# Routed experts in a transformer chain: items of one expert with both choices, against items of one choice at two experts

## The chip, the cores and the metric

The kernel runs on 1 core of a Trainium2 chip. TensorE (PE in the profile) does matrix products, VectorE (DVE), ScalarE (ACT) and GpSimd (POOL) do the rest, and SyncE (SP) and POOL issue the DMAs. The metric is device time in microseconds; the kernel before takes 2097.72 us, the median of three runs.

## The reference, cut to what matters

Four entries of 512 tokens with 128 features pass through a chain of attention and feed-forward blocks. The block that is changed is the second feed-forward, a mixture of eight experts with two choices per token and a capacity of 320 tokens for each choice at each expert:

```python
T = B * S                                      # 2048 tokens
probs = softmax(xf @ gate_w.T)
top_p, top_i = top_k(probs, 2)
w = top_p / (sum(top_p) + 1e-9)
capacity = int(1.25 * T / 8)                   # 320
oh = one_hot(top_i, 8)
my_rank = sum((cumsum(oh, axis=0) - 1) * oh, -1)   # rank within the choice
keep = my_rank < capacity
comb = einsum('tk,tke->te', w * keep, oh)
for e in range(8):
    y = silu(xf @ gate_proj_w[e].T) * (xf @ up_proj_w[e].T) @ down_proj_w[e].T
    out = out + comb[:, e:e + 1] * y
x = x + out
```

Behind it comes cross attention ("unit 3" in the kernel), which begins with a layer norm of x, entry by entry.

## The kernel before, in words

The whole chain is one program. `program_order` writes the order of all steps by hand as nested lists, and `interleaved` weaves neighbouring items into one flat list. Every engine walks the same list and does its own part of each step, so a step's place in the list sets its place on each engine. Buffers are rings (`T.slot`, `T.freed`); the ring `prob` has six buffers, `wide` (PSUM) three, `ys` three.

Tokens are routed through DRAM. After the gate of an entry, POOL scatters its normed tokens (`scatter`, L2181) to rows of `slots_in`, where expert e owns `ES` = 640 rows, 320 for first and 320 for second choices; tokens over capacity go to spare rows. When all four entries are scattered, the experts run as eight items, one expert each: SP loads the 640 rows (`slots_in`, L783), PE turns them (`f1_turn`), PE multiplies with the gate and up weights in four tiles of 320 columns (`f1_hidden`), ACT applies silu (L2016), DVE multiplies (L1671), PE projects down (`f1_down`, five blocks of 128 rows, two matmuls each), DVE copies the result to SBUF (L1678) and SP stores it to `slots_out` (L789). When all eight are stored, POOL gathers for entry 0, tile by tile, the rows of first and second choice (`gather`, L2201), and DVE adds them, scaled by their share, to x (`f1_add`, L1692), two adds per tile. Entries 1 to 3 follow inside the items of unit 3 (`prepare` in `cross_steps`), eight gathers and eight adds each. For entry 0, PE waits for the last gather before it runs some matmuls on an identity (`stay_awake`) and then turns the normed tokens. In front of the experts, the order has the keys and values of unit 3 for all entries (`kv_project`, DVE L1408 to L1439).

## Time and profile before

| | |
|---|---|
| times of three runs | 2097.72, 2096.28, 2105.15 us |
| median | 2097.72 us |
| the profiled execution: span of its instructions | 2100.9 us |
| PE busy | 1827.5 us, 87% |
| DVE busy | 1415.5 us, 67% |
| ACT busy | 1067.7 us, 51% |
| POOL busy | 784.6 us, 37% |

The profile comes from one more execution, for which the span from first to last instruction is listed and no other time. Busy time is summed over the whole program; the routed experts and what follows them lie between about 415 and 570 us. A matmul of 32-bit numbers shows as two records with a weight load (PEld) each. In the order of time, a row gives the start, the duration, the engine and line, what is written from what, the count, and in brackets how long the engine had been idle and what ended the idling.

### The profile page before, as it was taken

Reading aid. Unit: us, or ns where it says so; the run is one execution under the profiler, and the core shown is the slowest. Engines: PE = TensorE matmul, PEld = TensorE weight load, DVE = VectorE, ACT = ScalarE, POOL = GpSimd, SP = SyncE. Lnnn points to the kernel's source line nnn. Section 1 sums busy time; section 2 is a strip of 40 time slices with the busy share of each in tenths; the row PEclk is TensorE's granted clock in tenths of the full one; section 3 lists DMA queues with packets and bytes.
Section 4 is the critical chain, followed back from the end, with each engine's and each line's share of the span. In section 5 each row is a group of like instructions: output and inputs, shape, how many; then the busy total and the mean of one; then the engine's idle time right before and its main releaser. Section 6 shows DMA issues by size and latency. Waiting matters only on the chain. (4 is left out here: it accounts for less than half of the span.)

```text
span 2100.9 us, 34690 instructions
## 1 busy us (share of the span) xinstructions
PE 1827.5 (87%) x13011; PEld 1120.1 (53%) x13011; DVE 1415.5 (67%) x3427; ACT 1067.7 (51%) x1523; POOL 784.6 (37%) x1131
## 2 busy tenths in 40 slices
PE   5978998594777898899999999999999989989978
PEld 4557664373544444564544565644555554456557
DVE  8667776543676877864577885567786467787475
ACT  2655655131453566564466566366656446656510
POOL 4423324403624453431455342245443155443130
PEclk9999999597787898998999999999999999999989
DMA  7443333121000000141000033000014000003200
GB/s 227 111 137 101 109 104 97 63 69 39 21 1 13 1 1 13 37 110 43 16 1 1 1 93 84 28 1 1 1 44 120 14 16 2 1 26 99 52 1 21
DMA packets 69995, 100.91 MB, mean 48 GB/s; under 512 B 17126, under 2 KB 35438, under 8 KB 69188
## 3 DMA queue, kind: packets, MB, share of 16 engines
q1 hardware_dynamic: 60612, 90.01, 14.9%
q0 software_dynamic: 9216, 8.69, 1.6%
q8 instruction: 104, 1.70, 0.3%
q14 instruction: 63, 0.52, 0.1%
HBM read 52.43 MB, written 12.38 MB: 31 GB/s over the span
## 5 line engine op out<-in xcount | busy, mean ns | idle before, releaser
L1806 DVE TENSOR_REDUCE maxima<-wide 128x2 f32<-128x512 f32 (+3 forms) x512 | 406.1, 819 | 134.2 <-PE wide L836 130.7
L2042 ACT ACTIVATE prob<-wide 128x768 f32<-128x768 f32 (+1 forms) x384 | 332.2, 881 | 149.7 <-PE wide L836 149.4
L1965 ACT ACTIVATE prob<-wide 77x1024 f32<-77x1024 f32 x256 | 257.8, 1017 | 89.8 <-PE wide L836 86.5
L836 PE MATMUL wide<-q_g 32*128 32x256 f32 (+3 forms) x2048 | 268.5, 394 | 37.5 <-ACT prob L2042 18.1
L2284 POOL TENSOR_SCALAR_AFFINE_SELECT prob<-prob 128x256 f32<-128x256 f32 (+1 forms) x384 | 184.9, 487 | 296.4 <-ACT prob L2042 294.6
L1482 DVE TENSOR_REDUCE maxima<-wide 128x8 f32<-128x616 f32 x256 | 202.9, 795 | 110.7 <-PE wide L836 106.7
L836 PEld LDWEIGHTS wide<-q_g 32*128 32x128 f32 x2048 | 140.0, 188 | 205.6 <-issue 100.1
L2106 POOL TENSOR_TENSOR rstd<-moments,cst 128x4 f32<-128x4 f32 x88 | 90.4, 1027 | 360.7 <-DVE moments L1370 173.8
L1886 ACT ACTIVATE q_g<-wide 128x1024 fp32r<-128x1024 f32 x128 | 131.1, 1024 | 179.3 <-PE wide L836 177.4
L1886 ACT ACTIVATE q_g<-acc 128x512 fp32r<-128x512 f32 x192 | 114.5, 596 | 144.0 <-PE acc L836 139.0
L2191 POOL DMA_DIRECT2D masked_k<-kx x224 | 121.2, 546 | 177.4 <-PE wide L836 176.3
L836 PE MATMUL wide<-kx,q_g 128*128 128x312 f32 x512 | 178.0, 413 | 9.7 <-DVE maxima L1482 7.1
L836 PE MATMUL wide<-masked_q,masked_k 109*77 109x512 f32 x448 | 154.1, 429 | 11.9 <-DMA masked_q<-q_g 5.6
L836 PE MATMUL wide<-bias_q,ident_b 128*128 128x312 bf16 x448 | 134.8, 308 | 21.5 <-DVE maxima L1482 17.5
L836 PE MATMUL wide<-cst,hid 128*128 128x128 f32 x768 | 117.3, 293 | 30.6 <-DVE maxima L1482 9.8
L836 PE MATMUL acc<-prob,vx 77*32 77x512 f32 x1024 | 139.2, 616 | 0.7 <-ACT prob L1965 0.6
L836 PE MATMUL acc<-prob,A 128*32 128x512 f32 (+3 forms) x1408 | 136.1, 461 | 0.0
L836 PE MATMUL acc<-cst,hid 128*128 128x128 f32 x768 | 120.7, 281 | 13.8 <-DVE hid L1473 13.8
L836 PE MATMUL wide<-causal_b,ident_b 128*128 128x128 bf16 (+1 forms) x768 | 126.6, 248 | 0.0
L836 PE MATMUL wide<-hT,ffn_w 128*128 128x512 f32 x256 | 120.9, 597 | 3.9 <-DVE hid L1816 3.9
L836 PEld LDWEIGHTS wide<-cst,hid 128*128 128x128 f32 x768 | 91.5, 149 | 55.0 <-issue 21.1
L836 PEld LDWEIGHTS wide<-kx,q_g 128*128 128x128 f32 x512 | 101.4, 203 | 17.8 <-DVE maxima L1482 9.1
(253 smaller groups left out, 3096.1 us busy)
## 6 DMA issues: line engine op xcount, KB each, us to landing
masked_q<-q_g SPq DMA_DIRECT2D x448, 64.0 KB
masked_q<-mask_l SPq DMA_DIRECT2D x84, 308.0 KB
masked_k<-kx POOLq DMA_DIRECT2D x224, 19.5 KB, 1.9
A<-in_w SPq DMA_DIRECT2D x2, 2048.0 KB, 12.2
unit_w<-in_unit_w SPq DMA_DIRECT2D x8, 448.0 KB, 3.9
ffn_w<-in_ffn_w SPq DMA_DIRECT2D x4, 768.0 KB, 4.7
slots_in<-v_third SPq DMA_DIRECT2D x1, 2560.0 KB, 12.6
prob<-slots_in SPq DMA_DIRECT2D x8, 320.0 KB, 3.1
```

The costliest lines, as they stand in the source:

```text
L836: return e.matmul(out, lhsT, rhs, start=start, stop=stop, is_transpose=turn)
L1482: e.tensor_reduce(maxima[g % 2][:, 2 * half:2 * half + 2, :], v, AX.X, ALU.max, negate=True).then_inc(*made("max", ("free", tile)))
L1806: e.tensor_reduce(top[:, t, h], v[:, :, at0:at0 + P * t + P], AX.X, ALU.max, negate=True).then_inc(*made("max", *([("free", tile)] if t == ...
L1886: return e.activation(out, src, ACT.Copy, bias=0.0, scale=1.0)
L1965: e.activation(p[0:SC, :], s[0:SC, :], ACT.Exp, bias=0.0, scale=1.0).then_inc(*made("exp", pb, ("free", tile)))
L2042: e.activation(pv, sv, ACT.Exp, bias=0.0, scale=8 ** -0.5).then_inc(*made("exp", pb, ("free", tile)))
L2106: e.tensor_tensor(rstd[T.slot("rstd", held)][:, :], mo[:, 8 * NI:9 * NI], const("minus_half"), ALU.pow).then_inc(*made("rstd", held))
L2191: e.dma_start(masked_k[at][0:HR, :, i, :].bitcast(F32), kx[HR * i:HR * i + HR, i, 2 * half:2 * half + 2, SK * b:SK * b + SK].bitcast(F32)) ...
L2284: e.affine_select(out=v, in_=v, compare_op=ALU.is_ge, fill=0.0, base=0, pattern=[[0, many], [1, P]], channel_multiplier=-1).then_inc(*made ...
```

## The change: what it does

Items are grouped by choice. Items 0 to 3 hold first choices, items 4 to 7 second choices, and each holds two experts (`pair_of`), 320 rows of one expert on partitions 0 to 63 and 320 of the other on 64 to 127. `slots_in` and `slots_out` become two DRAM tensors each, one per choice. The scatters of an entry do the four first choices and then the four second ones. The first-choice rows of all entries are gathered behind the stores of items 0 to 3 and added to x in the order of the steps behind item 5 and later; the second choices follow where both were before. The sizes of loads, stores and matmuls change as the diff shows.

```diff
-SLOTS = E8 * ES
-SPARE = 2 * B * S
+HALF = P // 2
+SLOTS = E8 * CAP
+SPARE = B * S
...
-    every += [[[[("slots_in", x)]], [[("f1_turn", x)]], [[("f1_hidden", x, c, h)] for c in range(2) for h in range(2)],
+    sparse = [[[[("slots_in", x)]], [[("f1_turn", x)]], [[("f1_hidden", x, c, e)] for c in range(2) for e in range(2)],
                [[], [("f1_down", x)], [("f1_out", x)]]] for x in range(E8)]
-    every += [[[]]] * 3
-    every += [[[[("gather", 0, i)] for i in range(NI)]]]
+    sparse += [[[[]]] for _ in range(4)]
+
+    for b in range(B):
+        first_choice = sparse[E8 // 2 + 3 + b]
+        first_choice[0] = beside(first_choice[0], [[("gather", b, 0, i)] for i in range(NI)])
+        sparse[E8 // 2 + 4 + b][0] = beside(sparse[E8 // 2 + 4 + b][0], [[], [], [], [("f1_add", b, 0, 0)]])
+    sparse[-1][0] = beside([[("gather", 0, 1, i)] for i in range(NI)], sparse[-1][0])
+    every += sparse
...
+        def pair_of(x8, e):
+            return 2 * (x8 % (E8 // 2)) + e
...
+                    for k in range(2):
+                        e.dma_start(slots_in[k][0:SLOTS, :].rearrange("(p c) d -> p c d", p=P),
+                                    blank.unsqueeze(1).broadcast_to([P, SLOTS // P, D])).then_inc(*landed("clear_slots"))
...
+                for w in need(*[("scattered", b, x8 // (E8 // 2)) for b in range(B)], T.freed("prob", ("xs", x8))):
+                    e.wait_ge(*w)
+                e.dma_start(to[0:HALF, 0:ES], slots_of(x8, 0, slots_in)).then_inc(*landed(f"load_slots{x8}"))
+                e.dma_start(to[HALF:P, 0:ES], slots_of(x8, 1, slots_in)).then_inc(*landed(f"load_slots{x8}", ("xs", x8)))
...
+                of = ys[T.slot("ys", ("ys", x8))]
+                e.dma_start(slots_of(x8, 0, slots_out), of[0:HALF, :]).then_inc(*landed(f"store_slots{x8}"))
+                e.dma_start(slots_of(x8, 1, slots_out), of[HALF:P, :]).then_inc(
                     *landed(f"store_slots{x8}", ("stored_slots", x8), ("free", ("ys", x8))))
...
-                s, v = wide[T.slot("wide", tile)], xT[T.slot("xT", held)][:, EH * h:EH * h + EH]
+                s = wide[T.slot("wide", tile)]
+                v = xT[T.slot("xT", held)].rearrange("p (i q) -> p i q", i=EC)[:, :, HALF * n:HALF * n + HALF]
...
                 for i in range(EC):
                     for c in range(2):
-                        i_mm = mm(s[:, P * i:P * i + P], h[:, c, P * i:P * i + P], down1[:, x8, c, :], start=c == 0,
-                                  stop=c == 1)
+                        for n in range(2):
+                            at0 = EH * n + HALF * i
+                            i_mm = mm(s[HALF * n:HALF * n + HALF, P * i:P * i + P], h[:, c, at0:at0 + HALF],
+                                      down1[:, pair_of(x8, n), c, :], start=c == 0, stop=c == 1)
...
+            def gather(b, k, i):
+                held, t = ("got", b, k), NI * b + i
+                half = range(E8 // 2 * k, E8 // 2 * k + E8 // 2)
+                for w in need(*[("stored_slots", x8) for x8 in half], T.freed("prob", held)):
+                    e.wait_ge(*w)
+                e.indirect_dma_start(prob[T.slot("prob", held)][:, P * i:P * i + P], None, slots_out[k][:, :],
+                                     bass.IndirectOffsetOnAxis(slot[:, k, t:t + 1], 0)).then_inc(
+                    *landed(f"gather_first{i}" if (b, k) == (0, 1) else f"gather{b}_{k}", held,
+                            *[("got", b, k, j) for j in ([i] if (b, k) == (0, 1) else range(NI))]))
```

How the order moves, first on DVE, at the end of the experts. `hid<-wide,hid` are the products of `f1_hidden`, `A<-wide` the copies of `f1_down`, `x<-prob,comb,x` the scaled adds. The kernel before, from the copy of item 4:

```order
L1678 COPY A<-wide 128x640
L1671 TENSOR_TENSOR hid<-wide,hid 128x320 x4
L1678 COPY A<-wide 128x640
L1671 TENSOR_TENSOR hid<-wide,hid 128x320 x5
L1678 COPY A<-wide 128x640
L1671 TENSOR_TENSOR hid<-wide,hid 128x320 x2
L1678 COPY A<-wide 128x640
L1692 SCALAR_TENSOR_TENSOR x<-prob,comb,x 128x128 x2
L1351 BN_STATS moments<-x 128x6
```

The changed kernel, same place:

```order
L1697 COPY A<-wide 128x640
L1690 TENSOR_TENSOR hid<-wide,hid 128x320 x4
L1697 COPY A<-wide 128x640
L1690 TENSOR_TENSOR hid<-wide,hid 128x320 x2
L1710 SCALAR_TENSOR_TENSOR x<-prob,comb,x 128x128 x4
L1690 TENSOR_TENSOR hid<-wide,hid 128x320 x3
L1697 COPY A<-wide 128x640
L1690 TENSOR_TENSOR hid<-wide,hid 128x320
L1710 SCALAR_TENSOR_TENSOR x<-prob,comb,x 128x128 x4
L1690 TENSOR_TENSOR hid<-wide,hid 128x320
L1697 COPY A<-wide 128x640
L1710 SCALAR_TENSOR_TENSOR x<-prob,comb,x 128x128 x9
```

Four adds of entry 0 and four of entry 1 now stand between products; those of entries 2 and 3 stand behind the last copy, ahead of the first second-choice add.

On POOL, from the last scatters to the query operations of entry 2 (`prob<-slots_out,comb` are gathers). Before:

```order
L2181 DMA slots_in<-hn,comb 9216x128 x16
L2201 DMA prob<-slots_out,comb 128x128 x8
L2106 TENSOR_TENSOR rstd<-moments,cst 128x4
L2201 DMA prob<-slots_out,comb 128x128 x4
L2130 MEMSET hid 128x64x8
L2133 COPY hid<-hid 128x64x8
L2137 MEMSET hid 128x64
L2138 COPY hid<-cst 128x64
L2201 DMA prob<-slots_out,comb 128x128 x4
L2148 TENSOR_TENSOR x<-x,unit_w 128x512
L2106 TENSOR_TENSOR rstd<-moments,cst 128x4
L2201 DMA prob<-slots_out,comb 128x128 x6
```

The changed kernel:

```order
L2198 DMA slots_in<-hn,comb 4608x128 x16
L2217 DMA prob<-slots_out,comb 128x128 x20
L2123 TENSOR_TENSOR rstd<-moments,cst 128x4
L2217 DMA prob<-slots_out,comb 128x128 x2
L2147 MEMSET hid 128x64x8
L2150 COPY hid<-hid 128x64x8
L2154 MEMSET hid 128x64
L2155 COPY hid<-cst 128x64
L2217 DMA prob<-slots_out,comb 128x128 x2
L2165 TENSOR_TENSOR x<-x,unit_w 128x512
L2123 TENSOR_TENSOR rstd<-moments,cst 128x4
L2217 DMA prob<-slots_out,comb 128x128 x3
```

The first row of gathers holds sixteen of first choice and four of second, the later ones half of what they held.

On PE, a down projection and its neighbours, one piece of the difference:

```order
-L836 MATMUL wide<-A,hid 128x128 x10
+L852 MATMUL wide<-A,hid 64x128 x20
```

Each item has twenty matmuls of 64 output partitions in place of ten of 128; the other matmuls of an item keep their number and size.

## Rows read from the trace of the kernel before

**Rows 1.** The page: span, and busy time of each engine.
```profile
span 2100.9 us, 34690 instructions
PE 1827.5 (87%) x13011; PEld 1120.1 (53%) x13011; DVE 1415.5 (67%) x3427; ACT 1067.7 (51%) x1523; POOL 784.6 (37%) x1131
```
**Rows 2.** Windows: stretch, its length, busy us of each engine, granted clock, DMA share, GB/s.
```profile
core 0: us, PE busy (x) PEld busy (x) DVE busy (x) ACT busy (x) POOL busy (x), PEclk, DMA share, GB/s
...
434.00:477.00 43.00, 43.00 (x247) 34.84 (x246) 16.75 (x30) 14.65 (x31) 0.00 (x0) 1.00 0.23 77
...
486.00:503.00 17.00, 0.00 (x0) 0.00 (x0) 3.53 (x10) 0.00 (x0) 7.70 (x8) 0.57 0.17 50
503.00:570.00 67.00, 47.08 (x228) 29.48 (x229) 43.31 (x119) 22.98 (x28) 43.33 (x65) 0.78 0.09 24
```
**Rows 3.** PE in order of time, in a steady item of the experts.
```profile
448.63 2.39 PE L836 MATMUL wide<-A,hid 128*128 128x128 f32 x20
450.86 3.13 PE L836 MATMUL wide<-hT,A 128*128 128x320 f32 x11
```
**Rows 4.** Narrow windows, and PE in order of time, at self-attention values of 32 partitions.
```profile
802.22:802.36 0.14, 0.14 (x6) 0.13 (x8) 0.02 (x1) 0.14 (x1) 0.00 (x0) 1.00 0.00 0
...
802.23 0.42 PE L836 MATMUL acc<-prob,v_third 128*32 128x128 f32 x8
802.59 0.84 PE L836 MATMUL wide<-q_g 32*128 32x384 f32 x4
```
**Rows 5.** DVE in order of time, from the last products to entry 0's last adds.
```profile
482.57 0.49 DVE L1671 TENSOR_TENSOR hid<-wide,hid 128x320 f32<-128x320 f32 x1 [0.58 <-ACT hid L2016]
485.71 0.82 DVE L1678 COPY A<-wide 128x640 f32<-128x640 f32 x1 [2.65 <-PE wide L836]
495.90 0.74 DVE L1692 SCALAR_TENSOR_TENSOR x<-prob,comb,x 128x128 f32<-128x128 f32 x2 [9.36 <-DMA prob<-slots_out,comb]
...
503.37 0.74 DVE L1692 SCALAR_TENSOR_TENSOR x<-prob,comb,x 128x128 f32<-128x128 f32 x2 [1.43 <-DMA prob<-slots_out,comb]
```
**Rows 6.** Stores: fourth in time, all by source with landing; first and eighth gather.
```profile
459.00 0.32 SPq L789 DMA_DIRECT2D slots_out<-A  x1
...
L789 SPq DMA_DIRECT2D slots_out<-A x8: 319/320/320, 437.7 to 486.6; - x8
...
DMA to landing us min/median/max: 2.1/2.2/2.5
...
491.88 1.01 POOL L2201 DMA_INDIRECT prob<-slots_out,comb  x1 [76.19 <-issue]
...
500.76 0.95 POOL L2201 DMA_INDIRECT prob<-slots_out,comb  x1 [0.30 <-issue]
```
**Rows 7.** PE in order of time: its first matmuls behind the experts.
```profile
503.32 3.60 PE L836 MATMUL wide<-ident_b 128*128 128x512 bf16 x8 [17.64 <-DMA prob<-slots_out,comb]
```
**Rows 8.** DVE in order of time: one small operation, adds of entries 1 to 3.
```profile
518.74 1.70 DVE L1297 TENSOR_SCALAR hid<-maxima 128x16 int32<-128x16 int32 x1
...
521.03 2.31 DVE L1692 SCALAR_TENSOR_TENSOR x<-prob,comb,x 128x128 f32<-128x128 f32 x8 [0.37 <-DMA prob<-slots_out,comb]
...
539.86 2.32 DVE L1692 SCALAR_TENSOR_TENSOR x<-prob,comb,x 128x128 f32<-128x128 f32 x8 [5.39 <-DMA prob<-slots_out,comb]
...
563.15 3.16 DVE L1692 SCALAR_TENSOR_TENSOR x<-prob,comb,x 128x128 f32<-128x128 f32 x8
```
**Rows 9.** The start of the experts in order of time, several engines.
```profile
414.73 0.96 POOL L2181 DMA_INDIRECT slots_in<-hn,comb  x1 [0.30 <-issue]
416.62 0.54 DVE L1408 SCALAR_TENSOR_TENSOR rope_b<-wide,cst,ubs 128x312 f32<-128x312 f32 x1 [3.87 <-remote]
417.05 1.75 SPq L783 DMA_DIRECT2D prob<-slots_in  x4
...
419.98 1.30 PE L836 MATMUL wide<-cst,prob 128*128 128x128 f32 x5 [8.54 <-DVE kx L1439]
...
426.47 6.52 PE L836 MATMUL wide<-hT,A 128*128 128x320 f32 x16 [3.14 <-DVE vx L1417]
```

102 lines of the change are left out of this document (44 added, 58 removed).

## The prediction

> **What bounds the kernel now.** I first read the page: TensorE (PE) is busy 87% of a span of 2100.9 us [rows 1]. That average hides the stage the diff touches, so I then cut the stretch around the routed experts into windows [rows 2]. The reader is to see two different kernels there. From 434 to 477 us PE is busy 43.00 of 43.00 us, at full clock, while VectorE (DVE) and ScalarE have half their time free: anything added to PE there is added to the end. From 486 to 503 us PE does nothing at all: 17 us of waiting. From 503 to 570 us it is busy 47 of 67 us: a stretch of chains and waits, in which PE time is not the price but every late operand is.
>
> Next I read the engines' order of time inside these windows. A steady item spends 2.23 us (448.63 to 450.86) on its 20 down-projection matmul records, 0.11 us each, the pace of PE itself [rows 3]. The idle 17 us are one chain [rows 5 and 6]: the last copy to SBUF ends at 486.53, the last store leaves at 486.57 and lands 2.1 to 2.5 us later (about 488.7), GpSimd (POOL) starts its first gather only at 491.88, issues eight gathers 1.27 us apart, the last from 500.76, and PE is released when that one lands [rows 7].
>
> **The change, part by part.** All deltas are made against the profiled execution; its span is 3.2 us above the median of 2097.72, inside the spread of the three times, so I carry the sum of deltas over to the median.
>
> *Gathers moved forward.* Only four second-choice gathers now stand before PE's restart. Four fewer at 1.27 us: -5.1 us. The sixteen first-choice gathers stand on POOL behind the stores of items 0 to 3. The fourth store leaves at 459.00 and lands by 461.5 [rows 6]; sixteen gathers at 1.27 us take 20.3 us, so they are over near 485 even if the first starts 3 us late. POOL has nothing else there, and the second-choice gathers have to wait for the last store anyway. Cost on the path: nothing; if they slipped by more than 4 us they would push the second ones.
>
> *The first gather's delay.* Between the landing near 488.7 and POOL's start at 491.88 lie about 3.1 us, though between gathers POOL idles only 0.30 us [rows 6]. Nothing else shows what it waits for. It was the first gather of the program. If the delay belongs to a first use, or to the eight store semaphores waited for together, it is now spent under the experts. The bounds are 0 and -2.8 us. I take -2.8, because the nearest rows, all later gathers, show 0.3; the rival below keeps the other end.
>
> *Scaled adds.* DVE does two per tile in 0.74 us, 0.37 each [rows 5]. Tile 3 needs one instead of two: -0.4 us. The four first-choice adds of entry 1 now stand between the last two products of item 7. The last product started at 482.57 after 0.58 us of idling [rows 5], so 1.5 us of adds make it 0.9 us late, and the last down projection with it: +0.9 us. Those of entry 0 stand in item 6 between products too, where a later product finds the same half microsecond of slack each time: +0.1. The adds of entries 2 and 3 (eight, 3.0 us) run while the last store and the gathers are under way; if that cover were gone they would cost 3.0.
>
> *Two stores for one.* The 64-row halves need a second issue of 0.3 to 0.4 us behind the last copy: +0.4 us. The loads are doubled as well, but are issued items ahead of their use.
>
> *Down projection in two column halves.* Forty matmul records of 64 output partitions replace twenty of 128. No row of before has this shape. The upper bound is that they run one after another at today's 0.11 us: 4.46 us instead of 2.23, +2.23 per item, +17.8 us for eight. The lower bound is that the halves run side by side: +0. The nearest rows are the self-attention values, whose outputs are 32 partitions wide [rows 4]: eight records of 128 columns begin at 802.23 and the next work at 802.59, and within 0.14 us six matmul records are under way and all eight weight loads have been made. So column groups do run side by side: eight records took 0.36 us where in series they would need 0.89. Two rounds of four at the 0.11 us of rows 3 are 0.22, so 0.14 us goes to entering, leaving and spacing. An item of the changed kernel has twenty rounds of two. If the 0.14 comes once, it takes 2.37 us; if it comes with every two rounds, 3.6. I take 2.6, nearer the first, since entering and leaving come once: +0.35 per item, +2.8 in all, on the path, since PE is full there.
> The Trainium skill ("TensorEngine Tiling (Array Packing)", Key Properties) speaks against this part: a change of tiling mode drains the engine, and here the mode changes twice per item. The gap in rows 4 agrees in size with such a drain; it is inside my +0.35, and the sum is the same by page and by row.
>
> *Later entries.* Entries 1 to 3 need four adds instead of eight. Rows 8 give 2.31, 2.32 and 3.16 us for eight: -1.2, -1.2 and -1.6 us of DVE. Their gathers are halved too, so the waits ahead of these adds shrink: 0.37 us goes, and of the 5.39 us for entry 2 one gather fewer behind POOL's query operations and 0.4 us less ahead of them take about 1.7. That is 6.1 us of shorter chain. PE idles 20 of the 67 us there, so much of it should come through, but part meets other waits. I take 70%: -4.3 us.
>
> *Start of the stage.* The loads of items 0 to 3 now wait only for the first-choice scatters, which end four scatters (5 us) sooner. In before the first load leaves at 417.05 and PE turns at 419.98, but PE's hidden matmuls start only at 426.47, released by DVE's key and value chain, whose second copy stood until 416.62 on a wait the profile calls remote [rows 9]. The loads are not what comes last: I take 0, with -3.9 (that wait) as the other end.
>
> *Scatters, blanking.* As many rows, bytes and instructions, except that two blanking DMAs are four; they lie at 116 us, far from any reader: 0.
>
> Sum: -5.1 - 2.8 - 0.4 + 0.9 + 0.1 + 0.4 + 2.8 - 4.3 = -8.4 us, so 2097.7 - 8.4 = 2089.3 us.
>
> **The rivals.**
> (a) The halves run in series. 17.8 in place of 2.8 adds 15.0: 2104.3 us, slower than before. It decides from (8.4 + 2.8) / 8 = 1.4 us per item upward. For it: no 64-wide row exists, and twenty passes without a break are unlike the two of rows 4. Against it: rows 4 themselves.
> The Trainium skill ("TensorE: Matmul & The Clock Gate", The mechanism) says weight loads overlap running matmuls only where the row group differs, which column halves do not; loads laid bare would give this rival's outcome. Rows 4 show eight loads made while matmuls ran, which speaks against the page.
> (b) The 3 us before the first gather stay, since they belong to the store and not to POOL: 2092.1 us. For it: a store's landing is the last event ahead of the gap. Against: the trace shows it landed.
> (c) Only the restart gains; entries 1 to 3 are held by the maxima and POOL's query work: the -4.3 are lost, 2093.6 us. For it: other waits stand in the same stretch.
> (d) Other waits go too: the remote wait of 3.9 us at the start (scatters and DVE were active together), and the 1.70 us that one small DVE operation took beside POOL work at 518.74 [rows 8]. 2089.3 - 3.9 - 1.5 = 2083.9 us.
>
> **How the numbers follow.** Forecast 42%; (a) 15%, (b) 12%, (c) 13%, (d) 13%; 5% for what I have not thought of, mostly slower. Half a per cent, 10.5 us, is about what a measurement of this kernel can tell from no change. The forecast lies just inside it: small errors put it on either side (15 of its 42 points beyond -10.5), (d) is faster, (b) and (c) are the same, (a) is slower than before but by 6.6 us only; a third of its chance, where (b) or (c) joins it, passes +10.5. That gives faster 0.30, same 0.59, slower 0.11. The range of 8 in 10 goes from 2081 (d with the halves free of cost) to 2105 (a).
>
> **What would show it.** Down projection: forty records within 2.7 us and an item period near 7.4 us; 4.4 us means (a). Gathers: sixteen on POOL between about 462 and 485 us, then four at once after the last store lands; a gap of 3 us there means (b). PE's idle stretch should shrink from 17.6 us to about 10. The wait ahead of entry 2's adds should fall from 5.39 us to under 4. I am wrong if an add waits for its first-choice gather and holds the products behind it on DVE, or if PE's hidden matmuls start elsewhere than near 426 us.

## The result, and the profile after

The changed kernel took 2079.93 us (median of 4 runs, 2073.79 to 2082.77), the kernel before in alternation on the same chip 2100.47 us (4 runs, 2096.28 to 2105.15): a ratio of 0.9897, 95% interval 0.9874 to 0.9921. It is 20.5 us faster. The forecast was 2089.3 with a range of 2081 to 2105, and 0.59 for "same". Four executions of each kernel stand behind the 20.5. Its two nearest relatives, measured ten times each further down, gained 14.7 and 12.4 us in their medians, so part of the 20.5 may be luck of the four.

The page of the changed kernel; beside [rows 1] busy time has hardly moved, and the span is 20.4 us shorter:

```profile
span 2080.5 us, 35033 instructions
...
PE 1828.3 (88%) x13166; PEld 1118.9 (54%) x13171; DVE 1412.0 (68%) x3427; ACT 1067.7 (51%) x1523; POOL 785.5 (38%) x1131
```

Its windows (columns as in [rows 2]). PE is full in the experts, as before; the last stretch holds 52.40 us of PE work instead of 47.08, and TensorE's granted clock there is 0.90 instead of 0.78. The windows stand at the same times and not at the same work, since PE restarts 14.4 us earlier now:

```profile
434.00:470.00 36.00, 36.00 (x282) 27.03 (x282) 15.27 (x30) 11.99 (x25) 10.70 (x12) 1.00 0.33 92
479.00:488.90 9.90, 0.00 (x0) 0.00 (x0) 4.08 (x14) 0.00 (x0) 3.80 (x4) 0.63 0.23 60
...
503.00:570.00 67.00, 52.40 (x306) 34.44 (x304) 50.00 (x136) 34.45 (x44) 28.74 (x49) 0.90 0.03 9
```

PE of the changed kernel in order of time: the first hidden matmuls (to [rows 9]), a down projection and what follows it ([rows 3]), and PE's first matmuls behind the experts, called the restart from here on ([rows 7]):

```profile
412.17 1.30 PE L852 MATMUL wide<-cst,prob 128*128 128x128 f32 x5 [4.41 <-DMA prob<-slots_in]
...
416.27 6.50 PE L852 MATMUL wide<-hT,A 128*128 128x320 f32 x16 [0.82 <-DVE vx L1436]
...
424.32 2.40 PE L852 MATMUL wide<-A,hid 128*64 128x128 f32 x40
426.65 3.50 PE L852 MATMUL wide<-hT,A 128*128 128x320 f32 x12
...
488.93 3.33 PE L852 MATMUL wide<-ident_b 128*128 128x512 bf16 x8 [10.96 <-DMA prob<-slots_out,comb]
```

SP's queue: the first load and the two issues of the last store; POOL: first and last of the sixteen first-choice gathers, first and last of the four second-choice ones ([rows 6]):

```profile
408.47 0.49 SPq L797 DMA_DIRECT2D prob<-slots_in  x1
...
478.85 0.45 SPq L804 DMA_DIRECT2D slots_out<-A  x1
479.34 0.60 SPq L805 DMA_DIRECT2D slots_out<-A  x1
...
455.95 1.01 POOL L2217 DMA_INDIRECT prob<-slots_out,comb  x1 [43.46 <-issue]
...
474.86 0.97 POOL L2217 DMA_INDIRECT prob<-slots_out,comb  x1 [0.30 <-issue]
482.71 0.95 POOL L2217 DMA_INDIRECT prob<-slots_out,comb  x1 [6.87 <-DMA slots_out<-A]
...
486.46 0.95 POOL L2217 DMA_INDIRECT prob<-slots_out,comb  x1 [0.30 <-issue]
```

DVE: the end of the gate, the first two key and value chains behind it, first and last copy, and the scaled adds ([rows 5, 8, 9]):

```profile
401.09 0.25 DVE L1678 TENSOR_REDUCE qkv<-qkv 128x16 f32<-128x64 f32 x1
...
401.72 0.54 DVE L1427 SCALAR_TENSOR_TENSOR rope_b<-wide,cst,ubs 128x312 f32<-128x312 f32 x1 [0.17 <-PE wide L852]
...
406.19 0.54 DVE L1427 SCALAR_TENSOR_TENSOR rope_b<-wide,cst,ubs 128x312 f32<-128x312 f32 x1
...
426.77 0.82 DVE L1697 COPY A<-wide 128x640 f32<-128x640 f32 x1 [1.39 <-PE wide L852]
...
478.00 0.82 DVE L1697 COPY A<-wide 128x640 f32<-128x640 f32 x1 [2.59 <-PE wide L852]
478.86 2.31 DVE L1710 SCALAR_TENSOR_TENSOR x<-prob,comb,x 128x128 f32<-128x128 f32 x8
485.27 0.35 DVE L1710 SCALAR_TENSOR_TENSOR x<-prob,comb,x 128x128 f32<-128x128 f32 x1 [4.10 <-DMA prob<-slots_out,comb]
...
503.03 1.14 DVE L1710 SCALAR_TENSOR_TENSOR x<-prob,comb,x 128x128 f32<-128x128 f32 x4
...
519.42 1.14 DVE L1710 SCALAR_TENSOR_TENSOR x<-prob,comb,x 128x128 f32<-128x128 f32 x4 [3.62 <-DMA prob<-slots_out,comb]
...
561.73 0.69 DVE L1721 TENSOR_REDUCE f_scale<-hn 128x4 f32<-128x512 f32 x1
```

**A ruler for all runs.** Five events exist in every kernel: DVE's last gate reduction (401.09 here), its first and last copy of a down projection (426.77, 478.00), PE's restart (488.93), and the first `f_scale` reduction behind unit 3 (561.73). They cut each kernel's one trace into four stages (us, start to start):

| kernel | A: gate to first copy | B: first to last copy | C: last copy to restart | D: restart to f_scale |
|---|---|---|---|---|
| before | 32.47 | 48.82 | 17.61 | 84.57 |
| changed | 25.68 | 51.23 | 10.93 | 72.80 |
| scatters alternating | 26.70 | 51.23 | 11.07 | 73.96 |
| before, column halves | 27.02 | 50.74 | 17.63 | 84.66 |
| gathers late | 25.53 | 50.74 | 14.87 | 82.38 |
| before, repeated | 28.64 | 48.82 | 17.67 | 84.75 |
| before, early gather | 34.91 | 48.82 | 15.38 | 84.51 |
| gathers forward | 35.01 | 68.01 | 11.06 | 73.43 |
| adds late | 34.98 | 67.52 | 11.07 | 71.62 |
| gathers doubled | 35.22 | 66.62 | 11.14 | 80.79 |
| changed again | 35.06 | 68.11 | 11.10 | 71.53 |
| paced | 35.02 | 56.09 | 10.99 | 74.80 |
| paced and warm | 35.32 | 54.18 | 10.82 | 72.84 |
| run at item 4, first chip | 27.26 | 48.82 | 15.31 | 83.05 |
| the same, another chip | 34.56 | 57.27 | 15.63 | 83.03 |

From before to changed that is -6.8, +2.4, -6.7 and -11.8 us: -22.8 in the four stages. What lies ahead of the gate ran 3.3 us shorter and what lies behind the last event 5.7 us longer, though the change touches neither.

### The profile page after: what moved, and what is told of

Read it like the earlier page. It is cut to its first block and busy times, and to the rows that moved or that the text cites. A ratio compares the mean times of both kernels' runs of the same rounds, so it can differ in the third digit from the quotient of the medians.

```text
span 2080.5 us, 35033 instructions
## 1 busy us (share of the span) xinstructions
PE 1828.3 (88%) x13166; PEld 1118.9 (54%) x13171; DVE 1412.0 (68%) x3427; ACT 1067.7 (51%) x1523; POOL 785.5 (38%) x1131
## 3 DMA queue, kind: packets, MB, share of 16 engines
q1 hardware_dynamic: 60900, 90.01, 15.2%
## 5 line engine op out<-in xcount | busy, mean ns | idle before, releaser
L852 PE MATMUL acc<-cst,hid 128*128 128x128 f32 x768 | 119.8, 280 | 13.5 <-DVE hid L1492 13.5
L852 PEld LDWEIGHTS wide<-kx,q_g 128*128 128x128 f32 x512 | 100.7, 201 | 14.8 <-DVE maxima L1501 5.2
```

Of the source, the lines that this page charges most:

```text
L852: return e.matmul(out, lhsT, rhs, start=start, stop=stop, is_transpose=turn)
```

## The experiments

Each diff below is cut to its main lines. The ratio behind a time is to the kernel before in alternation on the same chip, with its 95% interval.

**One part at a time** (four kernels beside each other; kernel before 2101.87 us). *Scatters alternating*: the changed kernel, its last first-choice scatter being the seventh of the last entry's eight instead of the fourth.

```diff
-                held, k = ("hn", "g1", 0, b), n // 2
-                for i in (2 * (n % 2), 2 * (n % 2) + 1):
-                    t = NI * b + i
+                held, i = ("hn", "g1", 0, b), n
+                t = NI * b + i
+                for k in range(2):
```

> The changed kernel, but the eight scatters of an entry alternate between first and second choice again, as before. In the traces, the hidden matmuls of item 0 start 22.05 us after entry 3's last gate reduction in the kernel before (404.42 to 426.47) and 15.18 us after it in the changed one (401.09 to 416.27). Theory: the loads leave as soon as the fourth instead of the eighth scatter of entry 3 is out; here the last first-choice scatter is the seventh, so loads leave three scatters later, 3 x 1.27 = 3.8 us, and the distance is 19.0 us; total 2084. Rival: the two stalls of DVE (3.2 and 3.8 us) belong to the alternating order of the scatters; then they come back and the distance is near 22, total 2087. Second rival: those stalls are chance, the loads were not what came last, and the distance stays near 15.

Measured: 2087.17 us, 0.9943 (0.9916 to 0.997). The first load leaves 11.48 us behind the gate's end instead of 7.38, PE's hidden matmuls start 2.5 us later, where 3.8 were expected, and stage A is 1.0 us longer.

*Before, with column halves* and nothing else:

```diff
-                        i_mm = mm(s[:, P * i:P * i + P], h[:, c, P * i:P * i + P], down1[:, x8, c, :], start=c == 0,
+                        for n in range(2):
+                            at = P * i + 64 * n
+                            i_mm = mm(s[64 * n:64 * n + 64, P * i:P * i + P], h[:, c, at:at + 64], down1[:, x8, c, :],
...
```

> The kernel before, with nothing changed but the down projection, whose twenty matmul records per item become forty of 64 output partitions (two column halves of the same expert). Theory: halves run side by side and each entry and exit costs 0.1 us, so the item period goes from 7.09 to about 7.39 us and the total up by 2.4 us. Rival: the higher period of the changed kernel comes from its split views or from its doubled loads and stores; then the period here stays 7.09. If the halves ran in series the period would be 9.3.

Measured: 2104.07 us, 1.0007 (0.9984 to 1.0031). Copies stand 7.39 us apart, as in the changed kernel, instead of 7.09: 0.30 per item. The halves account for all of it. (A copy is DVE's copy of a down projection, one per item; here and below, distances are from the start of one to the start of the next.) Stage A shrinks by 5.5 us here too, with the old loads and scatters: most of what stage A of before lost is not the change's to give.

*Gathers late*: layout, items and scatters as changed, but both choices gathered and added where before had them, tile by tile.

```diff
-    for b in range(B):
-        first_choice = sparse[E8 // 2 + 3 + b]
...
-    sparse[-1][0] = beside([[("gather", 0, 1, i)] for i in range(NI)], sparse[-1][0])
+    sparse[-1][0] = beside(sparse[-1][0], [[("gather", 0, 0, i), ("gather", 0, 1, i)] for i in range(NI)])
...
-            got = [[("gather", b + 1, 1, i)] for i in range(NI)] if b + 1 < B else []
+            got = [[("gather", b + 1, 0, i), ("gather", b + 1, 1, i)] for i in range(NI)] if b + 1 < B else []
```

> The changed kernel, but the first-choice gathers and adds stand beside the second-choice ones again, tile by tile as before; items by choice, halves, split scatters and stores stay. Theory: all of the gain behind the last product (18 us by the two traces) belongs to the gathers moved forward, so PE idles about 18 us again at the restart, the 3 us in front of the first gather are back, and the total is 2080 + 16 to 18 = 2097. Rival: part of the later gain (11 us from the restart to entry 3's adds, where 4.3 were forecast) is alignment of DVE with POOL and of the clock, not of the gathers; then the total is below 2092.

Measured: 2094.95 us, 0.9966 (0.9938 to 0.9994). One gather still slipped into the experts (it needs only the first four stores), so seven remained after the last store. Stages C and D grow by 3.9 and 9.6 us. Stage C agrees with the single prices found below: 17.61 before, + 0.77 for the second store issue, - 1.26 for the gather that slipped, - 2.3 for the first gather's gap, is 14.8, and 14.87 was measured.

*Before with an early gather*, first try:

```diff
+    every[-4][0] = beside(every[-4][0], [[("warm_gather",)]])
```

> The kernel before, with one more gather of 128 rows (from the expert inputs into a free buffer, its result unused) on POOL behind the last scatter, at the start of the experts. Theory: the 3 us between the last store's landing and the first real gather belong to the first gather of the program, so the extra one takes them and the first real gather starts within 0.5 us of the landing: total 2.5 to 3 us shorter. Rival: the 3 us belong to the wait for eight stores' semaphores or to the landing; then the gap stays and the total does not move.

Measured: 2097.41 us, 0.9988 (0.9964 to 1.0012). The new step was missing from the list of POOL's steps, so no gather was added: this is the kernel before once more, and tells only that a repeat agrees in B, C and D within 0.2 us, and that stage A does not repeat (28.64 against 32.47).

**The first gather, the order of the late gathers, and POOL's share** (another chip; kernel before 2112.91 us). *Before, early gather, mended*: one gather out of `slots_in` into a spare tile stands behind the scatters, and the real ones need it to have landed.

```diff
+            def warm_gather():
+                for w in need(*[("scattered", b) for b in range(B)]):
+                    e.wait_ge(*w)
+                e.indirect_dma_start(qkv[:, 0, 0:D], None, slots_in[:, :],
+                                     bass.IndirectOffsetOnAxis(slot[:, 0, 0:1], 0)).then_inc(
...
-                for w in need(*[("stored_slots", x8) for x8 in range(E8)], T.freed("prob", held)):
+                for w in need(("warm",), *[("stored_slots", x8) for x8 in range(E8)], T.freed("prob", held)):
```

> What the run with the extra gather was meant to be: the kernel before with one gather of 128 rows on POOL right behind the last scatter, into a free buffer (the spare rows of the expert inputs are blanked too, at 116 us; no output changes). In four traces the first gather starts 3.01 to 3.02 us after POOL's last wait is over, and a later gather that also waited for four stores starts 0.70 us after. Theory of a first use: the extra gather takes the 3 us at the start of the experts and the first real gather starts 0.7 us after its wait, 2.3 us sooner. Rival, a long pause: POOL has stood for over 40 us before each of those first gathers and for 6 us before the later one; then the gap is 3.0 us here too, since POOL stands for 65 us again.

Measured: 2112.2 us, 1.0003 (0.9984 to 1.0022). In its trace of POOL the added gather and the first real one:

```profile
421.33 1.05 POOL L2199 DMA_INDIRECT qkv<-slots_in,comb  x1 [4.35 <-issue]
493.24 0.97 POOL L2209 DMA_INDIRECT prob<-slots_out,comb  x1 [70.85 <-DMA slots_out<-A]
```

The real one now starts 3.92 us after the last copy instead of 6.17, and is put down to the store's landing: stage C falls by 2.2 us. POOL had stood for 70.85 us before it, so a long pause is not what costs the 3 us. Stage D is unchanged. The median doesn't show the 2.2 us; its interval ends at -3.4 us.

*Gathers forward*: second-choice gathers of entries 1 to 3 one to three rows earlier on POOL.

```diff
+            got = {t: [("gather", t, 1, i) for i in range(NI)] for t in range(1, B)}
+            ahead = {0: {3: got[1][:2], 6: got[1][2:3], 7: got[1][3:], 10: got[2][:2]},
+                     1: {3: got[2][2:], 8: got[3][:1], 9: got[3][1:2]}, 2: {3: got[3][2:3], 4: got[3][3:]}}.get(b, {})
```

> The changed kernel with the second-choice gathers of entries 1 to 3 issued one step further ahead: two of entry 1 in front of entry 0's norm instead of behind it (POOL idles 2.99 us there, two gathers are 2.5), two of entry 2 in front of entry 1's norm, and so on. Theory: the 3.62 us for which DVE waits ahead of entry 2's adds belong to its fourth gather, which stands behind POOL's query work; they go, and the distance from PE's restart to the first reduction of the experts behind unit 3 (72.8 us in the changed kernel, 84.6 before) falls by 2 to 3.5 us: total 2077. Rival: POOL's query work is what PE waits for in this stretch; gathers in front of it delay it and the distance stays or grows.

Measured: 2112.5 us, 0.9992 (0.9978 to 1.0006). Entry 2's adds come 1.6 us sooner after entry 1's than in the next kernel, entry 3's 4.0 later. Stage D was expected to fall by 2 to 3.5 us and is 1.8 to 1.9 longer than in the two kernels of this chip with the old order (*adds late*, *changed again*): moved, not gained.

*Adds late*: no scaled add between products.

```diff
-        sparse[E8 // 2 + 4 + b][0] = beside(sparse[E8 // 2 + 4 + b][0], [[], [], [], [("f1_add", b, 0, 0)]])
+        late = E8 // 2 + 4 + max(b, 2)
+        sparse[late][0] = beside(sparse[late][0], [[], [], [], [("f1_add", b, 0, 0)]])
```

> The changed kernel with the first-choice adds of entries 0 and 1 behind the last copy of the experts, with those of entries 2 and 3, instead of between products. Theory as forecast: the adds between the last two products delay the last down projection by 0.9 us; the distance of the last two copies, 6.38 us in the changed kernel and 5.77 before, falls to 5.9 (the 0.13 left being the column halves), and the sixteen adds (4.7 us) end before the second-choice gathers land 6.4 us after the copy, so the restart stays where it is behind the copy: total 0.5 us shorter. Rival: the adds run into the landing of the first second-choice gather and the restart comes later by as much or more.

Measured: 2108.09 us, 0.9982 (0.9964 to 1.0). The last two copies are 5.89 us apart; with the adds between the products they are 6.38: the adds cost 0.49.

*Gathers doubled*: the changed kernel, with a second gather from `slots_out[0]` into a spare tile behind each second-choice gather of entries 1 to 3. DVE's adds stay halved, POOL has before's number of gathers again.

```diff
-            got = [[("gather", b + 1, 1, i)] for i in range(NI)] if b + 1 < B else []
+            got = [[("gather", b + 1, 1, i), ("again", b + 1, i)] for i in range(NI)] if b + 1 < B else []
```

> The changed kernel with as many gathers on POOL in entries 1 to 3 as before: behind each second-choice gather one more of the same size into a spare buffer whose content nobody reads. DVE's adds stay halved. From PE's restart to the first reduction behind unit 3 it is 84.6 us in the kernel before and 72.8 us in the changed one. Theory: POOL's queue is the chain in this stretch, since its query operations stand behind the gathers; then 12 x 1.26 us more on POOL bring back most of the 11.8 us, all but the 3.5 us of adds, and the distance is 80 to 81: total 2088. Rival of the forecast: the gathers only shorten the waits ahead of the adds (2 us), the rest is alignment between DVE and POOL and the clock; then the distance is below 76.

Measured: 2119.83 us, 1.0028 (1.0007 to 1.0049). Stage D is 80.79 us: twelve gathers on POOL seem to give back 8.0 of the 11.8 us of the changed kernel, and 3.8 are left for the halved adds. Part of the 8.0 is TensorE's clock, as shown below.

**A wait that this chip brought.** On this chip the changed layout gained nothing, and stage B was 15 to 17 us longer. A wait that the other chip did not show is the reason; chips without it in the experts are called undisturbed below. *Changed again* is the changed kernel itself (kernel before 2109.48 us).

> The changed kernel, unchanged, a second time. In the last three runs, made on another chip on which the kernel before takes 2112.9 us (2101.9 on the first), DVE and ACT stood for 16.9 us in item 5 of the experts: both waited for the end of a down projection that PE had left at 481.6 us, both went on at 496.7, 2.9 us after POOL had issued its sixteenth gather in a row at 492.9. On the first chip none of this is in the changed kernel's trace. Theory: late delivery beside a long unbroken run of gathers is a property of the changed kernel that chips show in different measure. Then on a chip with the kernel before near 2113 the changed one takes 2107 to 2110, on one near 2101 it takes 2080 to 2085. Rival: the 15 us came with the three edits; then this run gains 18 to 22 us on any chip.

Measured: 2111.45 us, 1.001 (0.9989 to 1.0032). DVE, ACT and PE at item 5, and the first and the last of POOL's sixteen gathers:

```profile
481.24 0.49 DVE L1690 TENSOR_TENSOR hid<-wide,hid 128x320 f32<-128x320 f32 x1 [1.13 <-ACT hid L2033]
498.10 0.82 DVE L1697 COPY A<-wide 128x640 f32<-128x640 f32 x1 [16.37 <-remote]
...
480.77 0.44 ACT L2033 ACTIVATE hid<-wide 128x320 f32<-128x320 f32 x1 [0.38 <-issue]
498.16 0.77 ACT L2033 ACTIVATE hid<-wide 128x320 f32<-128x320 f32 x2 [16.96 <-remote]
...
480.66 2.40 PE L852 MATMUL wide<-A,hid 128*64 128x128 f32 x40
483.00 0.54 PE L852 MATMUL wide<-hT,A 128*128 128x320 f32 x1
483.86 2.14 PE L852 MATMUL wide<-hT,A 128*128 128x320 f32 x7 [0.33 <-issue]
498.98 1.43 PE L852 MATMUL wide<-hT,A 128*128 128x320 f32 x2 [12.98 <-DVE A L1697]
...
475.38 1.01 POOL L2217 DMA_INDIRECT prob<-slots_out,comb  x1 [53.25 <-issue]
...
494.30 0.95 POOL L2217 DMA_INDIRECT prob<-slots_out,comb  x1 [0.30 <-issue]
```

PE leaves the down projection at 483.00 and goes on. DVE's copy of it starts only at 498.10. ACT's next operation needs the hidden tile that PE made right behind it, and starts only at 498.16. They go on within 0.1 us of each other and 2.9 us after the end of the last gather (495.25); PE runs dry behind them. The sixteen gathers themselves keep their 1.26 us.

*Paced*: adds late, and first-choice gathers of entry b wait for b more stores, so that they come in groups of 8, 4 and 4.

```diff
-                half = range(E8 // 2 * k, E8 // 2 * k + E8 // 2)
+                half = range(E8) if k else range(E8 // 2 + b)
```

> The changed kernel with the adds of entries 0 and 1 behind the last copy, and with the sixteen first-choice gathers broken into four groups: entry b's wait for the store of item 3 + b instead of item 3, so POOL stands about 2.4 us after each four. Theory: DVE and ACT are held until a run of gathers ends, so with runs of 5 us instead of 20 the hold is at most 5 to 8 us instead of 15: on a chip with the kernel before near 2113, 8 to 14 us shorter than the changed kernel; on one without the hold, within 1 us of it. Rival: the hold comes from the traffic or from PE alone; then the spacing changes nothing and the copies' distance in item 5 is 22 us again where the changed kernel has it.

Measured: 2097.22 us, 0.9936 (0.9913 to 0.9959). The distances between copies from item 4 on are 11.17, 8.34 and 7.04 us, where *adds late*, with its sixteen in one run, had 22.43, 9.65 and 5.89 on this chip, and the same order on a chip without the wait (*one per product*, below) 7.38, 7.92 and 5.89.

*Paced, two queues*: as paced, and the second half of the last store is issued by ACT.

> As the paced one, and the second half of the last store is issued by ACT beside SP's first half instead of behind it. In the changed kernel SP ends its last issue 1.94 us behind the last copy's start, 0.77 us later than before. Theory: the first second-choice gather and the restart come 0.6 us sooner, 10.4 us behind the last copy instead of 11.07. Rival: ACT's issue and landing take as long as SP's second one; no change.

Measured: 2099.23 us, 0.9937 (0.9912 to 0.9962). The last issue ends 1.35 us behind the last copy's start instead of 1.94 and PE restarts at 10.58 instead of 10.99: 0.4 us, below what the medians can tell.

**Is the run of gathers enough by itself?** A run is a row of gathers that POOL issues back to back. The kernel before, with twelve gathers into spare rows back to back after the stores of items 0 to 3 (*at item 4*) or after that of item 0 (*at item 1*); nothing else of the change.

```diff
+                for w in need(*[("scattered", b) for b in range(B)], *[("stored_slots", x8) for x8 in range(4)]):
+                    e.wait_ge(*w)
+                for t in range(12):
+                    e.indirect_dma_start(qkv[:, t // 3, D * (t % 3):D * (t % 3) + D], None, slots_in[:, :],
+                                         bass.IndirectOffsetOnAxis(slot[:, 0, t:t + 1], 0)).then_inc(
```

> The kernel before with nothing else than twelve gathers in a row on POOL (15 us of issuing, from the expert inputs into a free buffer, result unused; the spare input rows are blanked too) from the landing of item 3's store on. Theory: the hold of DVE and ACT comes from an unbroken run of POOL's gathers alone, whatever the items are; on a chip that shows it (kernel before near 2110), the distance of two copies around item 5 or 6 grows from 7.09 or 7.62 to 14 us or more, and DVE goes on 1.5 to 3 us after the last of the twelve. Rival: it needs the split items or their 64-row stores; then all distances stay below 8 us. On a chip without the hold no distance grows under either theory.

> As the run before it, but the twelve gathers start at the landing of item 0's store, three items earlier. Theory: the hold goes with POOL's run; the long distance moves to the copies three items earlier (item 2 or 3). Rival: it goes with a place in PE's or the others' instruction streams (in three traces the same pair of instructions was held, DVE's copy and ACT's silu of item 5); then nothing grows here, or again at item 5.

These went to a chip on which the kernel before took 2096.99 us. Measured: 2100.08 us, 1.0027 (1.0002 to 1.0052), and 2098.75 us, 0.9991 (0.9955 to 1.0027). No copy was late: distances of 7.09, 7.62 and 5.8 in both. Whether the wait moves with the run's place stays undecided, since nothing waited here. Stage C is 15.31 and 15.17 us: the early-gather gain once more.

With them went *gathers late* again and *one per product*, adds late with every first-choice gather held back to a product of DVE (`beat = None if k else ("f1_mul", E8 // 2 + b, i // 2, i % 2)`).

> The changed kernel with first-choice gathers and adds back behind the experts (as the third run), now with the paced ones on one chip. It has one gather in the experts. Theory: no distance of two copies is over 8 us on any chip, so on a chip with the kernel before near 2110 this variant, 15 us slower than the changed kernel on the first chip, is 0 to 3 us faster than it (2107). Rival: the long distance is there without the gathers too.

> The changed kernel with the adds of entries 0 and 1 late and each of the sixteen first-choice gathers behind one of the sixteen products of items 4 to 7, so that POOL issues one gather every 1 to 3 us instead of one every 1.26. With groups of 8, 4 and 4 three distances were still 3.8, 0.7 and 1.3 us longer than 7.39, 7.62 and 5.89. Theory: the hold needs gathers back to back; here all distances are back at 7.39, 7.9 and 5.9 and the time is 4 to 6 us below the paced one: 0.991 of the kernel before. Rival: every gather holds the others for some microseconds; then the extra distance stays or spreads over the items, and the time is that of the paced one or longer.

Measured: 2094.61 us, 0.9978 (0.9947 to 1.0009), stages C and D as in its first run; and 2084.62 us, 0.9947 (0.9917 to 0.9976). The holding back had next to no effect, since POOL was behind the products already: all but one of its gathers stayed 1.26 us apart. So the distances of 7.38, 7.92 and 5.89 tell of a chip without the wait and not of the edit, and this is the *adds late* kernel on an undisturbed chip: stages 25.75, 50.75, 11.11 and 73.12.

The last three went to a chip with the kernel before at 2110.62 us: *at item 4* again, *gathers late* a third time, and *paced and warm*, the paced kernel with a gather of its own behind the first-choice scatters.

> The kernel before with twelve gathers in a row from the landing of item 3's store on, a second time, since the chip of its first run showed no hold at all (DVE's first key operations stood 0.63 and 5.10 us behind the last gate reduction, as in the other traces without a hold; on chips with it they stood at 2.4 to 3.8 and 13.8 to 14.2). If this chip holds by that mark: theory, a run of gathers alone is enough, and one distance of two copies is over 11 us; rival, the split items are needed and all stay below 8. If it doesn't, the distances are 7.09 and 7.62 again and nothing is decided.

> The changed kernel with first-choice gathers and adds behind the experts, a third time. If this chip holds: theory, the experts' distances are all below 8 us, since POOL has no run there, and the time is 3 to 6 us below the kernel before, where the changed kernel gained nothing on such chips. If it doesn't: again 2 to 7 us below the kernel before. Rival: a long distance on a chip that holds.

> The paced kernel (adds of entries 0 and 1 late, entry b's first-choice gathers behind the store of item 3 + b) with one more gather of 128 rows, into a free buffer with its result unused, right behind the first-choice scatters, which takes the 3.0 us of the program's first gather; the spare input rows are blanked too. So the first four start 2.3 us sooner and no two groups touch. If this chip holds: the extra distances of the paced kernel (3.8, 0.7 and 1.3 us) fall below 3 us in sum, and the time is 0.991 of the kernel before. If it doesn't: as the changed kernel, the last group ending before the second-choice ones start, 0.990 to 0.994.

Measured: 2114.03 us, 1.001 (0.9986 to 1.0035); 2107.22, 0.9977 (0.9954 to 0.9999); 2104.59, 0.9967 (0.9946 to 0.9988). DVE, ACT and the last of POOL's gathers in the kernel before with twelve added gathers, which POOL issued from 470.94 to 485.78:

```profile
477.14 0.49 DVE L1671 TENSOR_TENSOR hid<-wide,hid 128x320 f32<-128x320 f32 x1 [1.13 <-issue]
484.39 0.82 DVE L1678 COPY A<-wide 128x640 f32<-128x640 f32 x1 [6.76 <-remote]
...
487.19 0.44 ACT L2016 ACTIVATE hid<-wide 128x320 f32<-128x320 f32 x1 [10.09 <-remote]
...
484.83 0.95 POOL L2199 DMA_INDIRECT qkv<-slots_in,comb  x1 [0.30 <-issue]
```

The same kernel that lost nothing on its first chip here has distances of 12.58 and 10.57 us: on such a chip the run alone is enough, without the new layout. Without a run (*gathers late*) the distances are 7.39 throughout. Here DVE goes on 0.44 us before the last gather starts and ACT 2.8 us after DVE, so the wait doesn't always end with the run. Groups of four (*paced and warm*) give 10.42, 7.65, 9.27 and 4.68, 3.4 us in sum above the 50.7 us without the wait. That misses what was expected of it (under 3 us), and so does its time: 0.9967 is no better than *gathers late* beside it (0.9977), which has no run at all.

## Why the prediction was wrong, and where it was right

**Restart (predicted -7.9 with the store, measured -6.7): right in mechanism.** The four gathers that are gone had cost 1.26 us each. The 3 us were the first gather's. Its gap, 3.0 us from POOL's last wait to its start, went under the experts, and the early gather alone took 2.2 to 2.3 us off the kernel before. Rival (b) falls. The prediction's -2.8 was 0.5 too much, and the second store issue cost 0.77 us (from 1.17 or 1.18 us behind the last copy's start to 1.94), not 0.4.

**Column halves (+2.8, measured +1.9 over the seven distances of stage B): right.** 0.30 us per item, where 0.35 was predicted. Rival (a) falls: *before, column halves* has the halves and nothing else. The 0.30 lie in thirds: the forty records start 2.33 us before the next work instead of 2.23, the four hidden records ahead of them 1.18 instead of 1.08, and the hidden block behind them takes 3.33 instead of 3.23. The second and third stand where the matmuls change from full to half width and back. The change of tiling mode that the prediction reckoned with costs no more than these 0.1 us each.

**Adds between products (+1.0, measured +0.49): right in mechanism.** *Adds late* takes them away and gets the 0.49 back.

**Later entries: the term that was mis-sized** (-4.3 predicted, -11.8 measured). The step that failed is "one gather fewer behind POOL's query operations". It counted what gathers cost the adds that wait for them. It did not count what waits for POOL's other work, and that work was late. POOL before, in entry 2's query operations:

```profile
553.61 0.95 POOL L2201 DMA_INDIRECT prob<-slots_out,comb  x1 [0.30 <-issue]
554.57 0.65 POOL L2209 MEMSET A<- 128x640 f32 x1
555.27 0.69 POOL L2130 MEMSET hid<- 128x512 f32 x1
556.02 0.67 POOL L2133 COPY hid<-hid 128x512 f32<-128x512 f32 x1
```

The copy starts without a wait: DVE had written its operand at 555.49, and POOL was what came late. The same copy for entries 0 to 2 waited 1.02, 0 and 0 us for DVE before, and waits 2.15, 3.35 and 2.43 us in the changed kernel: POOL is the early one now. *Gathers doubled* shows that POOL's queue is the main cause. It leaves DVE's adds halved, gives POOL its twelve gathers (15.1 us) back, and stage D is 8.0 us longer than in the changed kernel (9.2 to 9.3 against *adds late* and *changed again* on its own chip). Against the kernel before with the early gather on that chip it is still 3.7 us shorter. Those are the adds, close to the 4.0 predicted for them before the discount.

TensorE's clock has a part too. It falls to half (1.2 GHz) while PE stands still before the restart, and it comes back at different times in kernels whose steps in stage D are the same. The first 9 us from the restart, clock in the third number from the end: kernel before with a run at item 1, with a run at item 4, then *paced* and *adds late*:

```profile
506.41:515.41 9.00, 7.41 (x22) 3.84 (x23) 3.20 (x13) 0.60 (x1) 5.46 (x6) 0.50 0.10 25
498.58:507.58 9.00, 6.58 (x26) 2.94 (x26) 4.70 (x15) 0.60 (x1) 5.95 (x7) 0.82 0.11 29
...
512.24:521.24 9.00, 7.80 (x24) 4.04 (x25) 3.21 (x13) 0.60 (x1) 3.57 (x4) 0.51 0.06 16
523.35:532.35 9.00, 6.79 (x26) 3.02 (x26) 4.14 (x14) 0.60 (x1) 4.72 (x6) 0.78 0.06 16
```

The five traces with before's order in stage D and a clock of 0.50 there need 84.4 to 84.8 us for it, the two with 0.81 and 0.82 need 83.0: the low clock costs 1.4 to 1.7 us. The changed kernel had 0.84, the kernel before 0.50. *Gathers doubled* had 0.51; the two paced kernels, with 0.50 and 0.51 and no doubled gathers, need 73.8 and 74.8, so the twelve gathers themselves are worth 6.0 to 7.0 us. The 11.8 us are then, as an estimate from these traces, 6 to 7 for POOL's queue, 3.7 for the adds and 1.4 to 1.7 for the clock. The clock's part need not be the change's: it came back late in some traces with the changed kernel's 11 us of idling too.

**Start of the stage: a choice that failed as well** ("The loads are not what comes last: I take 0"). Stage A is 6.8 us shorter, for two reasons. One isn't the change: before's traced execution held DVE twice at the key and value chains beside the scatters (3.22 and 3.87 us [rows 9]). Four other kernels with before's loads and scatters (two of them *before, repeated* and *before, column halves*), run on undisturbed chips, lack both waits and have stage A at 27.0 to 28.6. The other is: where those waits are gone, before's loads do come last. PE of the kernel before with a run at item 4, where the first work behind the load waits for it and the hidden matmuls follow without a gap:

```profile
423.14 2.37 PE L836 MATMUL wide<-cst,prob 128*128 128x128 f32 x10 [9.29 <-DMA prob<-slots_in]
425.33 5.23 PE L836 MATMUL wide<-hT,A 128*128 128x320 f32 x16
```

In the changed kernel the first load leaves 5.3 us sooner behind the gate, and the hidden matmuls begin 15.2 us behind it instead of 17.9 to 18.3. There DVE's value chain releases them (416.27), so 2.2 to 2.6 of the 5.3 us bring nothing. By the first copy the lead is 1.3 to 3.0 us. Delaying the last first-choice scatter by three places gives 1.0 us back. Before's row was read as the chain that decides, while it was a disturbance that hid it.

**The rivals.** (c) falls with stage D. (d), given 13% at 2083.9, was nearest, and wrong in its prices: its 3.9 us were not the change's, but its small DVE operation did get shorter. Two of them were drawn out before (1.70 us at 518.74, 1.60 at 560.43); in the changed kernel none takes more than 0.62. How much of the 6 to 7 us of POOL's queue that makes is not shown. The forecast fell 9.4 us short of the time, and 12.1 short of the difference. Of the differences of the stages, the later entries make 7.5 and the start 1.3 to 3.0; the halves and adds came 1.4 cheaper than forecast, and the restart gave 1.2 less. A bolder choice would not have been enough for the later entries: even the whole 6.1 us of shorter chain is 5.7 below what was measured.

**The traced stages against the median.** The traces are one execution each. With stage A counted at -1.3 to -3.0, their stages say -17 to -19 us. The alternation says -20.5 with four executions each, and with ten each -14.7 for *scatters alternating* and -12.4 for *one per product*. All are more than the forecast's -8.4, so its miss is not luck, but how large the gain is on a chip without the wait stays open between these numbers. Behind the last event no step differs, yet that stretch takes 1505.9 to 1523.4 us in the twenty traces. TensorE's clock dips to half there for 3 to 27 us at a time, not at the same places in each execution. The three longest have a mean clock of 0.945 to 0.951, the three shortest 0.953 to 0.960. Whether the dips lengthen the stretch or only go with it was not tried. On undisturbed chips the same order repeats within 0.5 us in stages B and C, and within 1.6 us in D on any chip (71.5 to 73.1 for the changed order where the clock came back early).

## What to carry to other kernels

When a queue engine issues gathers between its compute steps, look whether those steps start without a wait: then every issue taken out of the queue is worth more than the wait of its reader. A wait that appears beside other engines' work in one traced execution is worth a second execution before a term is priced by it, for it may hide the operand that really comes last. Long runs of GpSimd gathers beside a full PE pipeline may be better broken into groups at the stores they depend on: the paced kernel kept a gain (0.9936) on a chip where the changed kernel had none (1.001). With groups of four on another such chip it was 0.9967, and on a chip without the wait neither was run.

## What the runs showed of the hardware

**DVE and ACT can be held beside a run of POOL's gathers.** On the two chips where the kernel before took 2109 to 2113 us, all ten profiles show it beside the scatters, and in the experts each one that has a run of gathers there; on the other chips, with the kernel before at 2097 to 2102, none of ten shows it in the experts and one beside the scatters (before's own). In the experts DVE waits for the end of a down projection that PE has left long ago, and ACT for the hidden tile behind it. Beside the run of sixteen they stand for 16.4 and 17.0 us, where they stand 1.4 and 2.9 to 3.2 in an undisturbed item, and go on together 2.9 us after the run. Beside the run of twelve it is 6.8 and 10.1 us, and DVE goes on before the run has ended. Beside groups of eight and four DVE stands 3.0 to 5.2 us. At the key and value chains, beside the scatters, DVE starts its second chain 13.5 to 15.5 us behind the gate's end on those chips, 12.2 in before's own trace and 5.1 in the nine others. That makes stage A 34.6 to 35.3 us there instead of 25.5 to 28.6, which is about what the kernel before is slower by on those chips, and it leaves nothing of the change's gain in stage A. POOL is not slowed, and PE goes on until it lacks an operand. Which part of the chip holds the signal stays open; whether it depends on the place of the run was not settled.
By the Trainium skill ("SBUF — State Buffer", Who interferes with whom) DVE and GpSimd share a port pair, and PE and ACT never wait on anyone. The first agrees with the small DVE operation of [rows 8] that took 1.70 us beside POOL's work. The second does not speak to ACT's 16.96 us, which were a wait for a signal and not an operation drawn out.

**The first gather of this program costs some 3 us once.** From POOL's last wait to its start it is 3.0 us in nineteen of the twenty traces, whether that is in the experts (455.95) or behind the scatters (421.33). In the twentieth, *paced and warm*, POOL still had scatters to issue behind that wait. There the first gather starts 4.3 us behind the wait, but only 0.30 us behind the last scatter, so the 3 us cost no idle time. For the later gathers that wait for a store the gap is 0.1 to 0.7 us.
